# Layer 2 of a four-layer graph network: a loaded and a fresh block taken side by side, with 14 one-hot buffers and the remainders shared by VectorE and GpSimd

## What is computed

```python
k = x @ W_key + b_key
q = x @ W_query + b_query
v = x @ W_value + b_value
gate = jax.nn.sigmoid(k[dst] + q[src])
msg = gate * v[src]
agg = jax.ops.segment_sum(msg, dst, num_segments=N_NODES)
return agg + x @ W_skip + b_skip
```

## Time and profile before

| | |
|---|---|
| three runs, median (lowest to highest) | 4477.22 us (4474.76 to 4493.06) |
| the profiled execution, its own time | 4485.66 us |
| its span in the trace | 4484.0 us |
| mean granted TensorE clock | 0.913 of full speed |
| PE busy | 3588.5 us (80%), 48,222 matmuls |
| DVE busy | 2581.5 us (58%) |
| POOL busy | 2442.5 us (54%) |
| ACT busy | 1709.6 us (38%) |
| layer 2's chunks, first sigmoid to last POOL subtraction | about 3370 to 4184 us |

### The profile page before, as it was taken

One profiled execution on the slowest core, in us unless ns is written; L12 is line 12 of the kernel. 1 busy time (PEld: TensorE's weight loads), 2 busy tenths in 40 slices (PEclk: granted clock), 3 DMA queues, 4 the chain that ended last, 5 costly groups with the idle time before them and its releaser, 6 DMA issues. The chain is left out here.

```text
span 4484.0 us, 125703 instructions
## 1 busy us (share of the span) xinstructions
PE 3588.5 (80%) x48222; PEld 3292.3 (73%) x48222; DVE 2581.5 (58%) x3516; ACT 1709.6 (38%) x2778; POOL 2442.5 (54%) x2291
## 2 busy tenths in 40 slices
PE   0666759999699999759989899999767777777396
PEld 0556658888699999758778888888557667667396
DVE  5989958888411110256666666666336666666502
ACT  0555569999400000133333333333224444444200
POOL 0181777777666666647777777777104444444100
PEclk9777679999899999979999999999859999999798
DMA  4554358898999999579888898889417777777596
GB/s 139 231 206 171 144 208 326 322 328 327 272 412 366 418 417 417 207 259 301 289 291 276 289 307 282 289 288 304 152 29 266 243 239 247 242 244 249 169 407 247
DMA packets 437225, 1212.62 MB, mean 270 GB/s; under 512 B 111451, under 2 KB 250698, under 8 KB 429863
## 3 DMA queue, kind: packets, MB, share of 16 engines
q1 hardware_dynamic: 331478, 919.45, 57.9%
q10 hardware_dynamic: 39406, 174.14, 9.6%
q0 software_dynamic: 66016, 114.12, 8.6%
HBM read 844.59 MB, written 364.93 MB: 270 GB/s over the span
## 5 line engine op out<-in xcount | busy, mean ns | idle before, releaser
L946 POOL DMA_INDIRECT feat_slot<-SK,sidx_p x900 | 1083.6, 1204 | 536.7 <-issue 375.4
L988 POOL DMA_INDIRECT arena<-tab_l_src,SK x864 | 897.6, 1039 | 346.5 <-issue 269.4
L870 POOL TENSOR_TENSOR arena<-arena 128x448 f16<-128x448 f32 x343 | 364.4, 1063 | 666.1 <-ACT arena L1771 666.1
L1291 PE MATMUL PS<-arena 128*128 128x192 bf16 (+1 forms) x7203 | 616.1, 248 | 108.3 <-DVE arena L2252 61.9
L1291 PEld LDWEIGHTS PS<-arena 128*128 128x128 bf16 x7203 | 607.1, 98 | 115.8 <-DVE arena L2252 62.1
L1458 PE MATMUL PS<-arena 128*128 128x128 f16 x4802 | 460.2, 223 | 132.4 <-DVE arena L2433 71.9
L1462 PE MATMUL PS<-arena 128*128 (+1 forms) x4802 | 439.5, 195 | 0.0
L1458 PEld LDWEIGHTS PS<-arena 128*128 128x128 bf16 x4802 | 313.0, 99 | 159.9 <-issue 146.1
L1390 PE MATMUL PS<-arena 128*128 (+1 forms) x4178 | 422.1, 225 | 0.0
L1764 ACT ACTIVATE arena<-PS,scale_i 128x448 f32<-128x448 f32 x343 | 217.6, 634 | 433.5 <-PE PS L1462 431.2
L1462 PEld LDWEIGHTS PS<-arena 128*128 128x128 bf16 x4802 | 378.6, 100 | 0.8
(11 more groups left out here) (299 smaller groups left out, 6464.8 us busy)
## 6 DMA issues: line engine op xcount, KB each, us to landing
arena<-slot_rows SPq DMA_DIRECT2D x343, 448.0 KB
arena<-cnt_t SPq DMA_DIRECT2D x147, 896.0 KB, 9.7
hots<-arena ACTq DMA_DIRECT2D x175, 672.0 KB
arena<-hots SPq DMA_DIRECT2D x175, 672.0 KB
arena<-cnt_t SPq DMA_DIRECT2D x147, 672.0 KB, 8.7
cnt_t<-arena SPq DMA_DIRECT2D x49, 1568.0 KB
cnt_s<-arena SPq DMA_DIRECT2D x49, 1568.0 KB
arena<-in_edge_attr_dram ACTq DMA_DIRECT2D x55, 937.5 KB
```

What stands on the lines that cost most here:

```text
L870: pool.tensor_tensor(halves[i][:, n:2 * n], gated[i], halves[i][:, 0:n], ALU.subtract).then_inc(msg_lo, 1)
L946: pool.indirect_dma_start(feat_slot, bass.IndirectOffsetOnAxis(ap=sidx_p[odd][:, n:n + 1].bitcast(u32), axis=0), fwin[h][:, t * D:(t + 1) ...
L988: pool.indirect_dma_start(qgot[n % 3][:, slot_of[t] * P:(slot_of[t] + 1) * P], None, tab_src[4], bass.IndirectOffsetOnAxis(ap=gidx[odd][:, ...
L1291: last = nc.tensor.matmul(PS[:, at:at + w3], ring[u % RING][:, of:of + P], esplit[:, (i * CH + w) * w3:(i * CH + w + 1) * w3], start=u == ...
```

## The change

The blocks are taken in pairs: 24 pairs of a loaded and a fresh block, chunk by chunk in turn (`MIX` = 14 steps s; even s is a loaded chunk, odd s a fresh one, `kind_of`), and the 49th block, loaded, alone at the end. In detail:

- `hots_c` has 14 buffers; chunk c of a loaded block uses 2c, of a fresh block 2c + 1, and buffers and semaphores are free again when that buffer's chunk of the pair before is added up.
- PE adds up three steps late (`LAG`), not two. Loaded blocks sum in one PSUM bank, fresh blocks in another.
- The remainder of a loaded chunk is now made by DVE (`second_half`), that of a fresh chunk by POOL as before. `halves` has 7 buffers of 1,792 bytes, `gated` still three, taken in turn by `(s + r) % 3`.
- ACT's sigmoid of step s waits for the remainder of step s - 3, which used the same `gated` buffer; before it waited for add_up of that chunk.
- DVE selects ahead: select_rows for step s + 4, select_sums for step s + 3. It also takes both blocks' sums out of PSUM by one reduction each (`keep`); ACT has no part in that any more.
- `mixed_pairs` writes three pairs out, loops 6 times over three pairs, and writes three more and the last block out.
- SP loads in the order of use, and stores both results of pair j - 2 after the third load of pair j.

The core of the diff:

```diff
+MIX = 2 * NC
+LAG = 3
-        hots_c = [carve(73.5 + 5.25 * c, HOTS, bf16) for c in range(NC)]
+        hots_c = [carve(kb, HOTS, bf16) for kb in [73.5 + 5.25 * i for i in range(9)] + [24.5, 29.75, 49, 54.25, 59.5]]
-        gated = [carve(122.5 + 3.5 * i, CH * D) for i in range(3)]
-        halves = [carve(124.25 + 3.5 * i, 2 * CH * D, f16) for i in range(3)]
+        gated = [carve(122.5 + 1.75 * i, CH * D) for i in range(3)]
+        halves = [carve(127.75 + 1.75 * i, 2 * CH * D, f16) for i in range(NC)]
...
+        fresh_in = hots_put
+        rest_made = relu_made
...
+        def mixed_pairs(eng, body):
+            for j in range(3):
+                body(j, 2 * j % 3, first=j == 0)
+            with eng.Fori(1, PAIRS_N // 3 - 1) as i:
+                for t in range(3):
+                    body(i * 3 + t, 2 * t % 3)
+            for j in range(PAIRS_N - 3, PAIRS_N + 1):
+                body(j, 2 * j % 3)
...
+        def wait_rest(eng, j, s):
+            kind, c = kind_of(j, s)
+            if kind == "slots":
+                eng.wait_ge(msg_lo, j * NC + (PLACES + c + 1))
+            else:
+                eng.wait_ge(rest_made, j * NC + (PAIRS_N * NCH + c + 1))
...
 (POOL)
-                    for c in range(NC):
-                        i = (c + odd) % 3
-                        pool.wait_ge(msg_hi, w * NC + (c + 1))
-                        pool.tensor_tensor(halves[i][:, n:2 * n], gated[i], halves[i][:, 0:n], ALU.subtract).then_inc(msg_lo, 1)
+                    for s in steps_of(j):
+                        if kind_of(j, s)[0] == "natural":
+                            to = halves[s % NC]
+                            pool.wait_ge(msg_hi, mixed_at(j, s))
+                            pool.tensor_tensor(to[:, n:2 * n], gated[(s + r) % 3], to[:, 0:n], ALU.subtract).then_inc(rest_made, 1)
...
 (PE)
+                    for s in steps_of(j):
+                        meet(j, r, s)
+                        if s >= LAG or not first:
+                            add_up(*before_that(j, r, s, LAG))
...
 (ACT, messages)
-                        act.wait_ge(agg_made, w * NC + (PLACES + c + 1 - turns))
+                        j3, _, s3 = before_that(j, r, s, 3)
+                        wait_rest(act, j3, s3)
...
 (DVE)
+                def second_half(j, r, s):
+                    n = CH * w_
+                    to = halves[s % NC]
+                    dve.wait_ge(msg_hi, mixed_at(j, s))
+                    V.tensor_tensor(to[:, n:2 * n], gated[(s + r) % 3], to[:, 0:n], ALU.subtract).then_inc(msg_lo, 1)
...
+                def body(j, r, first=False):
+                    for s in steps_of(j):
+                        gate(j, r, s)
+                        if s == 1 and not first:
+                            keep(j - 1, "slots")
+                        if s == 2 and not first:
+                            keep(j - 1, "natural")
+                        if kind_of(j, s)[0] == "natural":
+                            select_ahead(select_rows, j, s + 4)
+                        elif not last_pair(j):
+                            select_ahead(select_sums, j, s + 3)
+                        if s >= 2 or not first:
+                            j2, r2, s2 = before_that(j, r, s, 2)
+                            if kind_of(j2, s2)[0] == "slots":
+                                second_half(j2, r2, s2)
```

More of the change, by code:

```diff
@@ L1465, in meet @@
-                    last.then_inc(pre_made, 1)
[L1467 to L1471, removed]
-                    if c == 4 and later(w, 0, 1):
-                        pe.wait_ge(zb_kept, w + NS)
-                    pe.wait_ge(msg_lo, w * NC + (PLACES + c + 1))
-                    parts = halves[(c + odd) % turns].rearrange("p (s j f) -> p s j f", s=2, j=CH)
-                    o = PS[:, 3072 + half * 512:3072 + half * 512 + 2 * w_].rearrange("p (s f) -> p s f", s=2)
-                    for j in range(CH):
-                        last = nc.tensor.matmul(o, sumT[c][:, j * P:(j + 1) * P], parts[:, :, j, :],
-                                                start=c in (0, 4) and j == 0, stop=c in (3, 6) and j == CH - 1)
-                    last.then_inc(agg_made, 1)
@@ L1482, in body @@
-                def body(w, odd, j, kept, first=False):
-                    for c in range(NC):
-                        meet(w, c, odd, j, kept)
-                        if c >= 2:
-                            add_up(w, c - 2, odd)
-                        elif not first:
-                            add_up(w - 1, NC + c - 2, (odd - 1) % turns)
-                blocks(pe, body, turns)
-                for c in range(NC - 2, NC):
-                    add_up(NB - 1, c, 0)
+                    if not isinstance(j, int) or j > 0 or s >= 3:
+                        pe.wait_ge(pre_free, j * MIX + (NS * NC + s + 1 - 3))
@@ L1493, in fast_or_general, with body @@
+                def body(j, r, first=False):
+                    for s in steps_of(j):
+                        meet(j, r, s)
+                        if s >= LAG or not first:
+                            add_up(*before_that(j, r, s, LAG))
+                mixed_pairs(pe, body)
+                for s in range(NC - LAG, NC):
+                    add_up(PAIRS_N, 2 * PAIRS_N % 3, s)
             def fast_or_general(k):
@@ L2408, in body @@
-                def body(w, odd, j, kept, first=False):
-                    for c in range(NC):
-                        old = (w, c - 2, odd) if c >= 2 else None if first else (w - 1, NC + c - 2, (odd - 1) % turns)
-                        if old:
-                            gate(*old)
-                        if not kept:
-                            select_rows(w, c, j)
-                            select_sums(w, c, j)
-                        if c == 4 and not first:
-                            second_part(w - 1)
@@ L2423, in slots @@
+                select_rows(0, 1)
+                select_sums(0, 1)
+                select_rows(0, 3)
+                mixed_pairs(dve, body)
+                for s in range(NC - 2, NC):
+                    second_half(PAIRS_N, 2 * PAIRS_N % 3, s)
+                keep(PAIRS_N, "slots")
                 dve.wait_ge(agg_in, 16 * (m + 1))
```

208 lines of the change are left out of this document (120 added, 88 removed).

## The result

Both kernels were timed side by side on one chip, four executions each. The kernel before took 4475.99 us (median, 4460.95 to 4493.06), the changed one **4578.13 us** (4573.15 to 4596.6): a ratio of **1.0221, 95% interval 1.0187 to 1.0255**, so 2.2% slower. The prediction said slower and 4656 us with a range of 4563 to 4760. The sign was right and the time lies in the range, but only because the range was drawn down past the first rival (4589): the time lies there, and the loss is 102 us where 180 were forecast.

What follows compares the result with a forecast made beforehand. No engine was full, so a cycle of waits in layer 2 set the pace. 4485.66 + 116 - 5.5 - 1 + 2 gave 4597, less 8.4 for the median 4589, plus 67 for the clock 4656 us; range 4563 to 4760.

Steps and rivals of the forecast that it cites:

- the first rival: In layer 2 PE's granted clock holds despite the stops, so nothing is added for it: 4589 us, chance 0.29.
- The cycle: Layer 2, from one second_half's end to the next through PE, ACT, POOL and DVE: 5.20 us for two chunks, against 4.56.
- Two of its signs of being right: In layer 2, a pair without a jump takes 36.5 to 40 us; the stretches' clock lies between 0.8 and 0.95.
- The upper bound for the hold: POOL's subtraction blocks DVE operations with two SBUF operands for the whole of its 1.03 us; the lower bound was nothing.
- The pair: A loaded and a fresh block in layer 2: 7 x 5.20 + 0.38 = 36.8 us, +4.84, times 24 pairs +116.
- The small edits: Around layer 2's pairs: one PE loop jump fewer -5.5 us, last block -1, start +2; loads and stores nothing.
- The last block: Layer 2's final block, without fresh partner or POOL: 3.80 us for two chunks, 1.9 each instead of 2.03, so -1.
- the +2 at the start: At layer 2's start three DVE selections wait for the second and fourth load: between 0 and +5 us, taken as +2.
- The clock: PE stops about 2.0 us 168 times in layer 2; half bring a clock fall at 0.80 us each: +67.
- The term's upper bound: At most 168 x 1.4 = 235 us, if all PE work in layer 2's cycle always ran at 1.2 GHz.
- POOL and DVE side by side: POOL's subtraction and DVE's select_sums in layer 2 do not block each other: cycle 4.34 us, total 4445, chance 0.06.
- A cycle of 4.4 to 4.6: In layer 2 the change gives back exactly what it takes, if PE's links shorten: 4455 to 4500 us, chance 0.04.

Runs made afterwards that it cites:

- the early place: Changed kernel with DVE's second_half of a loaded chunk one step earlier, behind select_rows instead of behind select_sums: 4291.08 us, 0.9589 of the kernel before.

## Why the prediction was right, and where it was not

**The cycle.** Right, link by link: 5.20 us expected, 5.15 found. POOL is ahead of select_sums by the 0.03 us of the working, select_sums' median is 1.482 (1.4 to 1.5 expected), select_rows falls to 0.679 (0.67), add_up waits 1.75 us on the average (about 2), and sigmoids wait for DVE 165 times. Two of its signs of being right did not come: the pair is below 36.5 us, and the clock of the stage is 0.97, not 0.8 to 0.95. The experiments show that it is this cycle, and that both engines' waits on second_half are needed to see it: seven gated buffers alone leave it at 5.15, a lag of 4 alone at 4.25, both together at some 3.5, and an early second_half removes it.

**The upper bound for the hold.** The prediction took the whole of POOL's 1.03 for operations of which no row showed it. Right: 1.48 for select_sums, and 1.45 for second_half where that stood in its way.

**The pair.** 36.13 us instead of 36.8. Of the 0.67, 0.35 are the seven cycles shorter by 0.05, and the rest is the copy: it was added to the cycle with 0.38, but select_sums ends when POOL lets go, whether it started late or not. Behind a copy it takes 1.10 instead of 1.48:

```profile
3773.29 0.62 DVE L2461 TENSOR_TENSOR arena<-arena,PS 128x448 f32<-128x448 f32 x1 [0.68 <-ACT arena L1826]
3773.83 0.35 DVE L2506 COPY sd<-SD 128x196 bf16 x1
3774.21 1.10 DVE L2512 TENSOR_TENSOR arena<-sd,iota 128x896 bf16<-128x896 bf16 x1
```

24 times 0.67 is 16 us.

**The small edits.** The five pairs with a jump took 40.64 to 42.02 us, on the average 5.0 more than one without; one jump fewer was put at 5.5. The last block ran at 1.92 us for a chunk, as worked out (1.9). Of the +2 at the start nothing is seen: the first sigmoid starts at 3368.23, at 3370.46 before.

**The clock, the step that failed.** The term was +67, half of 168 stops at 0.80 us. Behind 10 of the counted 152 stops the clock fell, and a fall costs 0.47 us of a pair, or 0.80 by the forecast's price: 5 to 8 us. The sum with the measured sizes is 4485.66 + 24 x 4.19 - 5.5 - 1 + 5 = 4585 against the profiled 4579.48. The step was mis-sized in its share of falls, one in 15 and not one in two, which was taken from eight stops of layer 1 (1.64 to 2.05 us, four with a fall). What differs there was not tried by itself, so why the clock held here stays open; the runs show that the stop was 1.81 us and not the 2.0 forecast, that behind such stops the clock nearly always held, and that with second_half done twice it fell behind half of the stops over 2.2. The term's upper bound, 168 x 1.4, is worked out from no row: the 1.59 us of work at half clock would cost 1.59 more. The first rival, the clock holds, is what happened, and it had been given 0.29.

That the time fell into the range is therefore not to this term's credit. Without the +67 the same working gives 4589, 11 above the result, and those 11 are again two misses that partly cancel: the pairs were put 16 us too high, the falls that did come at nothing.

**The other rivals.** POOL and DVE side by side (4445): select_sums would have stayed near 0.61, and it is 1.48. A cycle of 4.4 to 4.6 did come, but in another kernel, with second_half ahead of select_sums (4.61 us, 1.0021).

**What the prediction did not see** is how near the gain lay. It treated the order on DVE as given. The links of the early place were all in its rows: select_rows is done 1.85 us after second_half, the next gate starts at 2.64. That idle stretch of 0.79 us (0.68 measured) was used only to show that the keeps cost nothing, and it is where second_half costs nothing too.

## What to carry to other kernels

Find, for each engine, the instruction whose end several other engines wait for, and put it first in its engine's idle time, never behind one that a third engine can hold up: moving one subtraction by one step here turned 2.2% slower into 4.1% faster. As long as the engine has idle time left, a hold costs nothing unless something awaited is queued behind it, so ask what stands behind the long operation before removing it. And where one instruction releases two engines, each with its own limit, relieving one of them alone may show nothing.

## What was not expected of the hardware

- How much the granted clock differs for stops that differ little: 10 falls behind 152 stops of 1.74 to 1.91 us in the changed kernel, 99 behind 167 stops with a mean of 2.25 us in the run with second_half done twice. In that run a stop behind a fall is the shorter one (64 stops under 2.2 us, 63 of them behind a fall), and still 48 of these 64 brought the next fall.
- Once no engine's wait is left, PE stops for nothing that the profile shows, about 0.9 us each: 48.7 us in 27 times in 580 us of the kernel with the early place, 28.4 of them in its five jumps, against 17.7 us in 5 times, all of them jumps, in 880 us of the changed one. The short ones often stand 12 to 14 us apart (3454.29, 3466.96, 3479.41, 3492.94); what they are stays open. In that state a jump of the loop was worth some 6 to 10 us.
- An operation that POOL holds ends with POOL's, 0.48 us behind it, whenever it was issued: 1.48 us when issued at once, 1.10 behind a copy of 0.35.
